# Attention with fused feed-forward on eight cores: a higher fill quota in the head loop and earlier weight loads

## The reference

```python
q, k, v = (xn @ W.T split into 16 heads of 128, for Wq, Wk, Wv)
scores  = einsum('bhqd,bhkd->bhqk', q, k) * 128 ** -0.5
attn    = einsum('bhqk,bhkd->bhqd', softmax(scores), v) @ Wo.T

base    = xn @ W_base.T + b_base
onehot  = one_hot(argmax(softmax(xn @ router_W.T)), 8)
h       = einsum('bsd,erd->bser', xn, A) * onehot[..., None]   # 8 experts, rank 16
y       = x + attn + base + einsum('bser,eor->bso', h, Bw) * 2.0
```

## Time and profile before

| | us |
|---|---|
| median of 2 runs | 1587.55 |
| the runs | 1583.61, 1591.5 |
| the profiled execution | 1579.82 |
| its span on core 6, first to last instruction | 1578.2 |
| spans of the eight cores | 1571.0 to 1578.2 |
| stage of x loads and statistics, to the first write of mb | 85.4 |
| first base product of head 0 | 212.9 |
| PE busy | 1249.5 (79% of the span) |
| ACT busy | 581.1 (37%) |
| DVE busy | 440.7 (28%) |

### The profile page before, as it was taken

One profiled execution on the slowest core, in us unless ns is written; L12 is line 12 of the kernel. 1 busy time (PEld: TensorE's weight loads), 2 busy tenths in 40 slices (PEclk: granted clock), 3 DMA queues, 4 the chain that ended last, 5 costly groups with the idle time before them and its releaser, 6 DMA issues.

```text
span 1578.2 us, 16693 instructions; the slowest of 8 cores (1571.0 to 1578.2 us)
## 1 busy us (share of the span) xinstructions
PE 1249.5 (79%) x5164; PEld 475.3 (30%) x5266; DVE 440.7 (28%) x746; ACT 581.1 (37%) x674; POOL 94.6 (6%) x88
## 2 busy tenths in 40 slices
PE   3505788887888788878888888888888888878887
PEld 1101233332323232323333333333333333323333
DVE  1384312223131213131212122222222222243345
ACT  3510034434343434343434343434344444460000
POOL 1000100000000000000000101010101010000110
PEclk8955699999899999999998989898989898998988
DMA  9800481423333332323232323242414142014986
GB/s 221 247 13 1 35 73 12 43 19 36 28 27 29 26 30 24 30 24 33 21 33 22 35 20 36 19 36 18 39 16 40 15 41 26 3 12 92 156 165 175
DMA packets 174789, 77.71 MB, mean 49 GB/s; under 512 B 168432, under 2 KB 168432, under 8 KB 172656
## 3 DMA queue, kind: packets, MB, share of 16 engines
q0 software_dynamic: 167504, 43.03, 31.3%
q1 hardware_dynamic: 4896, 25.21, 5.0%
q10 hardware_dynamic: 2304, 8.39, 1.3%
HBM read 111.26 MB, written 8.39 MB: 76 GB/s over the span
## 4 chain that ended last, share of the span: by engine, by line
PE 70%; DMA 9%; ACT 9%; DVE 7%; issue 5%; ACTq 0%; DVEq 0%; SPq 0%
PE PA L568 37%; PE PC L636 10%; PE PD L648 7%; DMA arena<-x 6%; PE SB L616 4%; DMA y<-arena 3%; PE SA L616 3%; DVE xn_s L375 1%; DVE arena L547 1%; DVE xn_s L366 1%; ACT arena L525 1%; ACT arena L580 1%; ACT arena L577 1%; ACT arena L586 1%; ACT arena L583 1%
## 5 line engine op out<-in xcount | busy, mean ns | idle before, releaser
L568 PE MATMUL PA<-xn_s,arena 128*128 128x512 bf16 x2335 | 649.0, 409 | 26.7 <-ACT arena L596 21.8
L631 DVE TENSOR_TENSOR arena<-arena 128x512 bf16<-128x512 bf16 x480 | 204.2, 425 | 591.0 <-ACT arena L622 590.2
L568 PEld LDWEIGHTS PA<-xn_s,arena 128*128 128x128 bf16 x2400 | 246.0, 103 | 346.3 <-issue 100.6
L622 ACT ACTIVATE arena<-SB,consts 128x512 bf16<-128x512 f32 x256 | 198.9, 777 | 266.0 <-PE SB L616 265.2
L622 ACT ACTIVATE arena<-SA,consts 128x512 bf16<-128x512 f32 x256 | 198.8, 777 | 188.7 <-PE SA L616 188.5
L636 PE MATMUL PC<-arena 128*128 128x512 bf16 x511 | 202.6, 396 | 58.5 <-DVE arena L547 17.7
L648 PE MATMUL PD<-xn_s,arena 128*128 128x512 bf16 x495 | 196.2, 396 | 20.3 <-ACT arena L675 17.4
L636 PEld LDWEIGHTS PC<-arena 128*128 128x128 bf16 x512 | 49.5, 97 | 266.4 <-issue 264.6
L616 PE MATMUL SB<-arena 128*128 128x512 bf16 x255 | 103.7, 407 | 0.4
L616 PE MATMUL SA<-arena 128*128 128x512 bf16 x255 | 98.9, 388 | 0.1
L274 POOL DMA_DIRECT2D arena<-wb x16 | 18.4, 1149 | 999.9 <-PE PA L568 907.2
(11 more groups left out here) (118 smaller groups left out, 674.9 us busy)
## 6 DMA issues: line engine op xcount, KB each, us to landing
arena<-x SPq DMA_DIRECT2D x16, 1024.0 KB, 10.3
arena<-wk POOLq DMA_DIRECT2D x16, 512.0 KB, 13.9
arena<-wq POOLq DMA_DIRECT2D x16, 512.0 KB, 11.3
arena<-wv POOLq DMA_DIRECT2D x16, 512.0 KB, 10.5
arena<-wb POOLq DMA_DIRECT2D x16, 512.0 KB, 7.3
arena<-wo POOLq DMA_DIRECT2D x16, 512.0 KB, 12.4
arena<-x SPq DMA_DIRECT2D x16, 512.0 KB, 6.0
y<-arena ACTq DMA_DIRECT2D x16, 512.0 KB, 6.8
```

The source lines that it names most:

```text
L568: last = t.matmul(PA[:, o0:o0 + w], lhsT=wbuf[:, par * W + c * dh:par * W + (c + 1) * dh], rhs=xn(c)[:, tok0 + o0:tok0 + o0 + w], start=(c ...
L622: return s.activation(p_ap(i), SBT[i % 2][:, 0:w], AF.Exp, bias=ck("shift"), scale=ck("scale"))
L631: return v.tensor_add(dst, dst, p_ap(i))
```

## The change

Four things are edited.

1. The wq, wk and wv slices of head 1 are issued at the very start, behind those of head 0, with `reads=["mb"]`. This line stands ahead of the place where `mb` is first written.
2. In head h, POOL issues wq, wk, wv for head h+2 instead of h+1, ahead of wb for head h+1.
3. The quota is worked out over NI - 3 = 29 iterations instead of 32. The stream has 160 counted matmuls, so it is 6 instead of 5 (h = 0 to 14).
4. The two ops for the low transposes of v get a lowest iteration, `(nT // 2) * NQ + 1` = 17, and the loop that takes items stops in front of an op whose iteration hasn't come.

```diff
@@ -277,6 +277,13 @@
         p.emit("gpsimd", wslice_dma(wv_s[:, 0:W], wv_d, 0, dh), writes=["wv0"], dma=True, dsem="wv0")
+        if H > 1:
+            p.emit("gpsimd", wslice_dma(wq_s[:, W:2 * W], wq_d, dh, dh),
+                   reads=["mb"], writes=["wq1"], dma=True, dsem="wq1")
+            p.emit("gpsimd", wslice_dma(wk_s[:, W:2 * W], wk_d, dh, dh),
+                   reads=["mb"], writes=["wk1"], dma=True, dsem="wk1")
+            p.emit("gpsimd", wslice_dma(wv_s[:, W:2 * W], wv_d, dh, dh),
+                   reads=["mb"], writes=["wv1"], dma=True, dsem="wv1")
@@ -594,8 +601,9 @@
-            items.append(("op", "tensor", vtlo, ["vfm", "eye", "@PA"], ["@PA"]))
-            items.append(("op", "scalar", vtlo_ev, ["@PA"], ["vt"]))
+            vmin = (nT // 2) * NQ + 1
+            items.append(("op", "tensor", vtlo, ["vfm", "eye", "@PA"], ["@PA"], vmin))
+            items.append(("op", "scalar", vtlo_ev, ["@PA"], ["vt"], vmin))
@@ -653,14 +661,16 @@
         for h in range(H):
             par = h % 2
+            if h + 2 < H:
+                np2 = (h + 2) % 2
+                p.emit("gpsimd", wslice_dma(wq_s[:, np2 * W:(np2 + 1) * W], wq_d, (h + 2) * dh, dh),
+                       writes=[f"wq{np2}"], dma=True, dsem=f"wq{np2}", fresh_ok=True)
+                (the same for wk and wv)
             if h + 1 < H:
                 npar = (h + 1) % 2
-                p.emit("gpsimd", wslice_dma(wq_s[:, npar * W:(npar + 1) * W], wq_d, (h + 1) * dh, dh),
-                       writes=[f"wq{npar}"], dma=True, dsem=f"wq{npar}", fresh_ok=True)
-                (the same for wk and wv)
                 p.emit("gpsimd", wslice_dma(wb_s[:, npar * W:(npar + 1) * W], wb_d, (h + 1) * 128, 128),
                        writes=[f"wb{npar}"], dma=True, dsem=f"wb{npar}")
@@ -683,7 +693,8 @@
-            quota = max((mmtot + NI - 1) // NI, 2) if mmtot else 0
+            nsl_ = max(NI - 3, 1)
+            quota = max((mmtot + nsl_ - 1) // nsl_, 2) if mmtot else 0
@@ -717,7 +728,10 @@
                 while stream and (stream[0][0] == "op" or stream[0][1] <= b):
-                    it = stream.pop(0)
+                    it = stream[0]
+                    if it[0] == "op" and len(it) > 5 and i < it[5]:
+                        break
+                    stream.pop(0)
```

More of the change, by code:

```diff
@@ L655, in build @@
             par = h % 2
+            if h + 2 < H:
+                np2 = (h + 2) % 2
+                p.emit("gpsimd", wslice_dma(wq_s[:, np2 * W:(np2 + 1) * W], wq_d, (h + 2) * dh, dh),
+                       writes=[f"wq{np2}"], dma=True, dsem=f"wq{np2}", fresh_ok=True)
+                p.emit("gpsimd", wslice_dma(wk_s[:, np2 * W:(np2 + 1) * W], wk_d, (h + 2) * dh, dh),
+                       writes=[f"wk{np2}"], dma=True, dsem=f"wk{np2}", fresh_ok=True)
+                p.emit("gpsimd", wslice_dma(wv_s[:, np2 * W:(np2 + 1) * W], wv_d, (h + 2) * dh, dh),
+                       writes=[f"wv{np2}"], dma=True, dsem=f"wv{np2}", fresh_ok=True)
             if h + 1 < H:
                 npar = (h + 1) % 2
-                p.emit("gpsimd", wslice_dma(wq_s[:, npar * W:(npar + 1) * W], wq_d, (h + 1) * dh, dh),
-                       writes=[f"wq{npar}"], dma=True, dsem=f"wq{npar}", fresh_ok=True)
[L660 to L663, removed]
                 p.emit("gpsimd", wslice_dma(wb_s[:, npar * W:(npar + 1) * W], wb_d, (h + 1) * 128, 128),
```

## The result

| | before | changed |
|---|---|---|
| median of all runs, us | 1585.83 (10 runs) | 1605.56 (11 runs) |
| the profiled execution, us | 1579.82 | 1600.5 |
| ratio to before, 95% interval | | 1.0124 (1.0094 to 1.0154) |
| spans of the cores in the profile, us | 1571.0 to 1578.2 | 1576.9 to 1598.9 |
| mean granted clock | 0.89 | 0.91 |

In both columns a few runs in which one die ran at a lower clock are left out of the ratio. The changed kernel is 1.2% slower, 20 us (15 to 24), where I had forecast 42 us, 2.6%. The direction was right, the size wrong by a factor of two. The median of 1605.56 us lies inside the range that I gave, 1590 to 1660, but only because that range took in the neighbouring rivals.

A forecast was written before the change was run, and what follows sets the result against it. The prediction took PE, with its stalls and low-clock stretches, as the bound. Loop +38 us and early slices +4 make +42 on the profiled 1579.8, so 1621.8, or 1630 us on the median's scale; range 1590 to 1660.

The forecast's parts named there:

- the five stalls a head: PE waits on PA: v transposes 3.5 us, head boundary 3.4, denominator 3.4, its broadcast 3.6, behind q 1.3.
- five thin ones at 0.97: Iterations 27 to 31, without stream items: paced by exponentials at 0.97 us each instead of 0.74.
- The boundary, 2.9 us: Between a head's last product and the next head's first base product: wait of 2.9 us instead of 3.4.
- The clock term: PE's low-clock stretches behind three stalls in a head: loss of 5.9 us kept, plus 0.4 us a head.
- The work term of +2.1 us: Each head's loop and boundary: work and waits go from 60.9 to 63.0 us, +2.1 us a head.
- rival 1: Stalls in the heads: the low clock shrinks, -0.8 us a head, 1580 us, no change; chance 0.20.
- the term times 15: Heads 0 to 14, taken as alike: +2.5 us each, +38 us in all.
- The low transposes' limit, POOL's order: Stream's iteration limit for v's low transposes and later heads' slice order on POOL: cost and gain zero.
- the early slices push the x tiles: At the start, three extra slices share the DMA engines with x loads: +4 us, bounds 0 and 14.
- Rival 4: Start: x tiles held up in full, +14 us instead of +4, 1640 us; chance 0.10.
- rival 5: Head's end: thin iterations run at 0.74 us after all, +1.6 us a head, 1616 us; chance 0.09.
- rival 3: Heads: a fourth low-clock stretch or second long one, +1.7 us a head more, 1649 us; both about 1675; chance 0.18.

The follow-up runs named there:

- e6_drop8: Kernel before with 8 matmuls fewer in each head's block behind the loop, heads 1 to 15; one run, 1581.6 us beside 1580.95.
- e1_early_only: Kernel before with only head 1's wq, wk, wv slices issued at the start; ratio 1.0091 to before.
- e2_quota_only: Kernel before with only the quota raised from 5 to 6; ratio 1.008 to before.
- e3_after_real_wait: Changed kernel with head 1's three slices issued behind the first write of mb; ratio 1.0079 to before.
- e5_slices_late: Kernel before with head 0's three slices issued behind the first write of mb instead of at the start; ratio 0.9952 to before.

## Why the prediction was right or wrong, point by point

- **PE sets the end, and the five stalls a head.** Right. The stalls for k, the broadcast and the transposes are in the changed kernel as they were.
- **2.03 us an iteration, five thin ones at 0.97, product 31 at 5.9 us behind the last item.** Right: 2.03, 1.93 a pair, 5.90. The loss of dense work while ACT catches up is real.
- **The boundary, 2.9 us.** It is 3.15. The row I took it from begins where the chain entered the product, not where the product began (1376.91 instead of 1376.75 in the timeline).
- **The clock term, 5.9 us kept and 0.4 added.** This is the step that failed: I had all three low stretches stay because the three stalls stay. The stalls did stay, but one low stretch went and one became half as long, and the clock's cost was 3.2 us. The work term of +2.1 us (+2.4 with the boundary as measured) was there too, and the clock gave 2.7 back. With 72.7 us of work and stalls before (78.6 less 5.9), 72.7 + 2.1 = 74.8, and 74.8 + 0.25 + 3.2 = 78.3, against 78.4 measured and my 81. My rival 1, to which I gave 0.20, had this mechanism and priced a head at -0.8; it was -0.1 in most heads. e6_drop8 shows the same from the other side: 1.7 us less work, a low stretch more, and no gain. In the loop I had 38 us. It was 10: +2.3 in head 0, +4.3 in head 1, one head of +3.9, and 0.6 in head 15, less 1 us in the others.
- **Heads are alike, hence the term times 15.** This was the deeper error. The trace of before had said it: heads 3 to 14 all lie within 0.1 us of 78.5 while head 1, with the same work, takes 74.4. Such equality among stalls, copies and clock changes should have made me doubt that the length is a free sum.
- **The low transposes' limit, POOL's order.** Right, both nothing; e1_early_only and e2_quota_only add up to 1.7%, against 1.24% for both with the new order, and e3_after_real_wait, which has order, limit and quota, costs what e2_quota_only does. So the runs show no cost of either.
- **reads=["mb"] isn't a wait, and the early slices push the x tiles.** Right in kind. The size was 9.3 us where I took 4, inside my bounds of 0 and 14. I had assumed that the slices fit partly into open time of the DMA engines. The runs with 0, 3, 4 and 6 slices show 2.7 to 4.3 us for each, so room that takes three slices for nothing did not exist. Of a slice's 6.2 us of engine time, roughly half counts. This term was too low by 5 us and the one for the loop too high by 28, so a part of one error hid a part of the other.
- **What mb waits for.** DVE's write of mb found the slices landed: the last of them had landed 78.3 us after its issue at 8.5, at about 88 us, and DVE's idle time before the write (2.22 us) is put down to PE, as in the earlier trace rows. The cost came by the x tiles. In the changed kernel ACT's last square starts at 84.14 us, 9.8 later than in the earlier trace rows (that square and DVE's first write of mb, core 4):

```profile
84.14 2.00 ACT L313 ACTIVATE arena<-arena,consts 128x2048 bf16<-128x2048 f32 x1 [1.93 <-DMA arena<-x]
...
96.51 1.23 DVE L345 CAST arena<-PA 128x1024 bf16<-128x1024 f32 x1 [2.22 <-PE PC L341]
```

- **The rule of the 16 shared engines** (the Trainium skill, "DMA: Bandwidth & Descriptors", section "Issuing engines are not separate DMA queues") was the right warning: the trace agrees, with x tiles landing in 6.6 us with no slice beside them and 12.4 us with six, and the mirror run (e5_slices_late, mb 10.6 us earlier) shows that the three slices of the kernel before already held up the x tiles.
- **Rivals.** Rival 4 (x tiles held up in full, +14) was nearer than my term for its part; rival 5 is out, the thin iterations took 0.97; rival 3 happened in one head of 14, with low stretches at 0.50 behind the boundary, the denominator and, for 6.6 us, the broadcast, and in the transposes (core 4, from 1083.3 us on; 82.4 us, mean clock 0.90).

What stays open: why a head is held at 78.5 us from -8 to 0 matmuls and for the quota of 6, moves freely at +8, and falls to 75.1 at -16. That the clock makes up the difference is shown by the windows: a low stretch more at -8, and 6 to 7 us of low clock fewer at the quota of 6. Which stall loses or keeps its low stretch, and by what rule, is not shown, and heads of 82.4 us came on six cores of e2_quota_only and not on two, with the same program.

## What to carry to other kernels

Where repeated pieces have one and the same length to a tenth of a us while the granted clock inside them changes, don't add a saving or a cost of a few us to each: here work and clock traded against each other (3.4 us less work gave nothing for its first half and all for its second, and 1.7 us more cost 1.4). Filling faster isn't better if it leaves a thin end that a slower engine paces; spread the work over the whole loop and put copies and their users into different iterations. And look at what a merged step waits for: one flush, which split two kinds of work that had no business waiting for each other, gained five times as much as this whole change cost.

## What the runs showed of the hardware that I had not expected

- The same stall of 3.4 to 3.6 us is followed by a low-clock stretch of 0, 3.4 or 6.7 us in kernels that differ by a few us of work a head (before: about 3 behind the denominator, 6.7 at the broadcast; changed: 0 and 3.4).
- Removing 1.7 us of PE work from a head of 78.5 us changed its length by nothing and its mean clock from 0.91 to 0.89, with a low stretch of 3.3 us where there had been none (e6_drop8).
- Splitting a merged PE step made an iteration of seven 512-column matmuls 1.51 instead of 1.60 us. That the 0.1 us is the price of a step's wait for the end of PE's own previous step is my reading of the weight loads, not shown by a run.
- A weight slice of 1 MB read and 512 KB written in 256-byte pieces delays the end of the x stage by 2.7 to 4.3 us when it is loaded beside the x tiles, and takes 48 to 64 us to land itself (medians of the pairs in e1_early_only).
